# The FFN's block of a Mamba layer accumulated onto its rows by ScalarE, with B, C and dt stored sooner at a chunk's end

## What is computed

```
u    = layernorm(x);  xi, z = split(u @ in_proj)             # 1024 -> 2 x 2048
xc   = silu(causal_conv4(xi))
dt_r, B, C = rmsnorm of the three parts of xc @ x_proj       # 64, 16, 16
dt   = softplus(dt_r @ dt_proj + dt_bias);  A = -exp(A_log)
h_t  = exp(dt_t * A) * h_(t-1) + dt_t * B_t * xc_t           # 2048 channels x 16 states
y    = (sum_n h_t * C_t + D * xc) * silu(z)
x    = x + y @ out_proj.T                                    # 2048 -> 1024
x    = x + layernorm(x) @ W.T + bias                         # W = scale * (code - 128), 32 codes a scale
```

## Time and profile before

| what | value |
|---|---|
| median of 3 runs | 4584.67 us (4584.44 to 4585.98) |
| the profiled execution | 4594.81 us |
| its span, first to last instruction | 4593.0 us |
| a middle step (places 2 to 6), first scan to first scan | 32.26 us |
| place 7 and place 0 at the edge from chunk 7 to chunk 8 | 36.45 us and 38.77 us |
| wx, wo and wz loads | 1024 KB each, one of each in a step |

### The profile page before, as it was taken

One profiled execution on the slowest core, in us unless ns is written; L12 is line 12 of the kernel. 1 busy time (PEld: TensorE's weight loads), 2 busy tenths in 40 slices (PEclk: granted clock), 3 DMA queues, 4 the chain that ended last, 5 costly groups with the idle time before them and its releaser, 6 DMA issues.

```text
span 4593.0 us, 77871 instructions
## 1 busy us (share of the span) xinstructions
PE 4293.4 (93%) x25632; PEld 3867.8 (84%) x25632; DVE 4157.9 (91%) x5745; ACT 3535.6 (77%) x8848; POOL 3887.0 (85%) x2894
## 2 busy tenths in 40 slices
PE   7688889999999999999999999999999999998879
PEld 6567778888888988889888898988988888897769
DVE  3898989989999999999999899999999999999871
ACT  3787788878888788787878778787888878887750
POOL 0898989989898898989889898998989899899870
PEclk9788999999999999999999999999999999998889
DMA  7545556565756657575575756657575665655442
GB/s 245 159 126 175 151 181 177 167 216 173 220 160 189 194 174 221 155 220 168 165 230 156 225 163 208 187 153 229 163 222 172 199 182 162 213 172 177 136 141 92
DMA packets 201348, 828.91 MB, mean 180 GB/s; under 512 B 25456, under 2 KB 34416, under 8 KB 151792
## 3 DMA queue, kind: packets, MB, share of 16 engines
q1 hardware_dynamic: 141296, 639.35, 38.6%
q0 software_dynamic: 41216, 151.01, 18.7%
q10 hardware_dynamic: 18432, 33.56, 1.9%
HBM read 634.57 MB, written 55.05 MB: 150 GB/s over the span
## 4 chain that ended last, share of the span: by engine, by line
PE 61%; POOL 19%; DVE 8%; issue 7%; DMA 2%; ACT 1%; SPq 1%; POOLq 0%; DVEq 0%; ACTq 0%
PE ys L646 14%; PE gx L626 12%; POOL dbx L494 12%; PE ys L606 12%; PE g L799 10%; PE g L721 7%; DVE hb L1416 5%; POOL half L518 3%; POOL half L512 3%; PE ys L636 1%; PE hb L901 1%; DMA b_scratch<-ssmT 1%; DVE gx L1298 1%; DMA ybuf<-in_wf_scales 1%; POOL hd L507 1%
## 5 line engine op out<-in xcount | busy, mean ns | idle before, releaser
L494 POOL TENSOR_TENSOR dbx<-dtx,bb 128x1024 f32<-128x1024 f32 x1024 | 2426.6, 2370 | 232.3 <-DVE hb L1416 184.0
L1416 DVE TENSOR_TENSOR_SCAN hb<-hb,dbx 128x512 f32<-128x512 f32 x2048 | 2497.0, 1219 | 43.7 <-POOL dbx L494 25.7
L1111 ACT ACTIVATE hb<-dt,a_neg 128x256 f32<-128x256 f32 x4096 | 1789.1, 468 | 66.3
L606 PE MATMUL ys<-half,ident 128*128 128x256 f32 x3072 | 832.6, 407 | 186.4 <-POOL half L512 105.3
L799 PEld LDWEIGHTS g<-wo,ybuf 128*128 128x128 f32 x7680 | 945.0, 198 | 34.3 <-issue 17.7
L799 PE MATMUL g<-wo,ybuf 128*128 128x128 f32 x7680 | 953.2, 281 | 8.4 <-issue 8.4
L646 PE MATMUL ys<-xnT,wz 128*128 128x256 f32 x4096 | 925.2, 385 | 5.2 <-DVE ybuf L1375 5.2
L626 PE MATMUL gx<-xnT,wx 128*128 128x256 f32 x3968 | 894.4, 383 | 24.7 <-issue 10.8
L646 PEld LDWEIGHTS ys<-xnT,wz 128*128 128x128 f32 x4096 | 782.8, 193 | 116.0 <-DVE ybuf L1375 10.8
L606 PEld LDWEIGHTS ys<-half,ident 128*128 128x128 f32 x3072 | 580.5, 200 | 330.8 <-POOL half L512 138.2
L626 PEld LDWEIGHTS gx<-xnT,wx 128*128 128x128 f32 x3968 | 748.7, 191 | 129.3 <-issue 14.3
(11 more groups left out here) (108 smaller groups left out, 3134.7 us busy)
## 6 DMA issues: line engine op xcount, KB each, us to landing
wz<-in_win SPq DMA_DIRECT2D x128, 1024.0 KB, 5.0
hd<-hd POOLq DMA_DIRECT2D x256, 512.0 KB, 5.2
wx<-in_win SPq DMA_DIRECT2D x124, 1024.0 KB, 5.0
wo<-in_wout SPq DMA_DIRECT2D x123, 1024.0 KB, 7.3
wf<-wf_scratch SPq DMA_DIRECT2D x113, 512.0 KB, 3.6
xc_scratch<-xcn ACTq DMA_DIRECT2D x128, 256.0 KB, 2.8
xcs<-xc_scratch SPq DMA_DIRECT2D x128, 256.0 KB, 5.2
bb<-bc_scratch SPq DMA_DIRECT2D x64, 512.0 KB, 8.6
```

The costliest lines, as they stand in the source:

```text
L494: nc.gpsimd.tensor_tensor(dbx[:, k % 2, :].rearrange("p (n t) -> p n t", n=NQ), dtx[:, S % 2, a, :].unsqueeze(1).to_broadcast([P, NQ, T]), ...
L606: mm = nc.tensor.matmul(ys[i // 3][:, 0:T], ident[:], half[:, n % PLACES, w * T:(w + 1) * T], start=False, stop=(i % 3 == 2 and w == 1), s ...
L1111: ins = nc.scalar.activation(h[:, m * T:(m + 1) * T], dt[:, j % 2, a, :], ACT.Exp, scale=a_neg[:, ds((2 * j + a) * N + 2 * v + m, 1)])
L1416: nc.vector.tensor_tensor_scan(h[:], h[:], dbx[:, k % 2, w * UW:(w + 1) * UW], 0.0, ALU.mult, ALU.add).then_inc(scans, 1)
```

## The change

Four things change together.

1. In place 7 the RMS norm's square and sums, and ScalarE's evacuation of dt, B and C, stand one or two units earlier. TensorE makes `out_proj(3)` and `dt_proj` ahead of `x_in_proj(1)` and the groups. SyncE stores and loads B and C ahead of the load of wx, which waits for `x_in_proj(1)`.
2. In place 0 each part of the output block waits for the y of its own channel tiles, no longer for all 16. The parts 0 and 1 stand between late group 3 and late groups 4 and 5; VectorE makes the last y of the chunk before after product 3 (before: after product 1), and the first of its own after product 12 (before: 11).
3. The FFN's block is accumulated onto its rows: ScalarE copies the block's rows (x2 with the bias) into g1 after unit 15 (`ffn_in`, semaphore `f_pre`), TensorE accumulates onto them, and ScalarE copies the result out in the next step after unit 3 (`ffn_out`, semaphore `f_out`). VectorE's add (`add_ffn`) is gone, except for the last two chunks' at the kernel's end.
4. In the middle places TensorE's order is as before.

```diff
@@ SyncE
-                        sp.wait_ge(f_add, after(PAIRS * (c - 2)))
+                        sp.wait_ge(f_out, after(PAIRS * (c - 2)))
                         sp.dma_start(out_rows[c - 3], x2_rows(1 - st.parity)).then_inc(out_st, 16)
...
-                    if nx.x_job(nx_last):
-                        load_pair(S + PAIRS + 2)
                     if last and st.inproj:
                         bc_rows(c + 1)
                         for q in range(2):
                             load_b(c + 1, q)
                             load_c(c + 1, q)
+                    if nx.x_job(nx_last):
+                        load_pair(S + PAIRS + 2)
@@ TensorE
                     def g1_after_f():
-                        pe.wait_ge(f_add, after(S - 2 * PAIRS))
+                        pe.wait_ge(f_out, after(S - 2 * PAIRS))
...
-                        if was.outproj:
-                            g1_after_o()
-                        else:
-                            pe.wait_ge(f_add, after(S - 1 - 2 * PAIRS))
+                        pe.wait_ge(f_pre, after(S - 2 * PAIRS))
                         for tt in range(TT):
                             for kk in range(KH):
                                 mm = nc.tensor.matmul(g1[:, tt * P:(tt + 1) * P], x2nT[:, kk, tt * P:(tt + 1) * P],
-                                                      wf[:, kk, :], start=(kk == 0), stop=(kk == KH - 1))
+                                                      wf[:, kk, :], start=False, stop=(kk == KH - 1),
+                                                      skip_group_check=True)
...
-                            if first:
-                                pe.wait_ge(y_ready, after(2 * c * PAIRS))
                             if was.ffn:
                                 g1_after_f()
                             else:
                                 g1_after_o()
+                        if first:
+
+                            pe.wait_ge(y_ready, after(2 * (c - 1) * PAIRS + (part + 1) * TILES // 4))
...
                     ffn()
-                    late_groups()
+                    if first and st.ffn:
+                        late_groups(3)
+                        out_proj(0)
+                        out_proj(1)
+                        late_groups(4, 5)
+                    else:
+                        late_groups(3, 4, 5)
@@ ScalarE
+            def ffn_out(S):
+
+                k = S - 2 * PAIRS
+                act.wait_ge(f_mm, after(k))
+                nc.scalar.copy(block_rows((k - 1) // PAIRS, (k - 1) % PAIRS), g1_block).then_inc(f_out, 1)
+
+            def ffn_in(S):
+
+
+                k = S - 2 * PAIRS
+                act.wait_ge(bias_acc, 16 * (k // PAIRS + 1))
+                act.wait_ge(o_add, after(S - PAIRS + 1))
+                nc.scalar.copy(g1_block, block_rows(k // PAIRS, k % PAIRS)).then_inc(f_pre, 1)
...
+                    if st.before(first).ffn:
+                        ffn_out(S)
                     silus()
...
                     norm1(1)
+                    rms_square()
...
                     norm1(3)
-                    rms_square()
...
                     unit(10)
+                    ss_out()
...
                     unit(11)
                     norm2(3)
-                    ss_out()
...
                     unit(15)
+                    if st.ffn:
+                        ffn_in(S)
@@ VectorE
-                    add_ffn()
                     scan(2)
                     product(1)
-                    late_y()
+                    if not (first and st.ffn):
+                        late_y()
                     scan(3)
                     product(2)
+                    if last:
+                        add_x_proj()
                     scan(4)
                     product(3)
+                    if first and st.ffn:
+                        late_y()
                     scan(5)
                     product(4)
-                    add_x_proj()
+                    if last:
+                        rms_sums()
+                    else:
+                        add_x_proj()
                     scan(6)
                     product(5)
-                    rms_sums()
...
                     product(11)
-                    y_gate(S, 0)
+                    if not (first and st.ffn):
+                        y_gate(S, 0)
...
                     product(12)
+                    if first and st.ffn:
+                        y_gate(S, 0)
                     add_out()
```

## The result

The changed kernel takes **4618.1 us** (median of 4 runs, 4615.0 to 4623.0) against 4584.6 before: ratio 1.0075, 95% interval 1.006 to 1.009. The forecast was 4588, no change; the time is 2 us outside its range and on the slower side.

What follows compares the result with a forecast made beforehand. No single engine was held to bound the kernel; two nearly equal loops, over ScalarE and TensorE, set the middle step. Terms +19.5, +12, -22, -2.5 and -2 gave +5, shaded by 2: 4588 us, range 4552 to 4616.

Steps and rivals of the forecast that it cites:

- ScalarE's copies: Places 1 to 6, chunks 2 to 14: two new copies add 0.25 us to each of 78 steps, +19.5 us.
- less 0.07 and GpSimd's 0.21: Middle step, second loop: slacks of ScalarE and GpSimd taken off the table load's 0.47 us delay, leaving 0.2.
- the first loop: Middle step, over ScalarE: exponentials 3, table load, exponentials 4, scan 4, product freeing unit 3's bank; grows by 0.24 us.
- Place 7: Chunk edge: TensorE's z projection waits for VectorE's gate, +0.9 us at each of 13 edges, +12 us.
- Place 0: Start of chunk: fewer waits win 3.2 us, the clock's fall takes 1.5; -1.7 us at 13 edges, -22 us.
- wo lands late: Rival, places 7 and 0: wx ahead of wo in full DMA queues leaves place 0 worth 0; 4612 us, chance 0.28.
- the point named: Place 0: wo decides once it lands after 2302.2, 3.8 us into the place; from there each us costs one.
- The clock holds: Rival, place 0: shorter TensorE waits keep the clock up, giving the full -3.2 us; 4570 us, chance 0.22.
- VectorE was the bound: Rival, middle steps: each of 78 steps loses 0.33 us instead of gaining 0.25; 4544 us, chance 0.14.
- The third sign of being wrong: Place 0: a ScalarE wait for the bias transfer, with VectorE behind it; the wait was costed at nothing.
- The last edge: Edge from chunk 14 to 15: -2 us, with chunk 15 and the end staying as they are.
- The 10 us between trace and median: Kernel before: profiled execution 4594.81 against median 4584.67; the difference of 10.1 us was taken to stay the same.

Runs made afterwards that it cites:

- the run that takes the waits away: The changed kernel with wo loaded ahead of wx in place 7: 4606.6 us, ratio 1.0054 to the kernel before.
- the second: The kernel before, unchanged, traced once more: 4583.1 us, ratio 1.0002, span 4575.4 us.

## Why the prediction was wrong, step by step

**ScalarE's copies (+19.5 forecast, +37.5 measured): the step that failed.** The copy's time was right (0.37 estimated, 0.372 measured), and so was the wait for the FFN ("2103.01, 0.47 after the load's old start"). Wrong were the slacks taken off it: "less 0.07 and GpSimd's 0.21". 0.47 without them is within 0.03 of the growth. The 0.07 was the gap between unit 4's exponentials and scan 4, 0.12 in that step, less a hand-over of 0.04; but 0.10 us is that gap also in the changed kernel, where scan 4 plainly waits for ScalarE, and in no step of either trace is it smaller. At this scan it is the hand-over itself, although the gap comes down to 0.03 at scans of other units. The 0.21 was scan 9's end to GpSimd's next product less 0.13; this gap is 0.34 before and 0.35 after in middle steps, although the step grew by 0.5. It was no slack: GpSimd could not have followed sooner, as it was in its own work.

```profile
2116.60 1.27 POOL L518 TENSOR_TENSOR half<-hc 128x512 f32<-128x512 f32 x1
2117.82 2.37 POOL L494 TENSOR_TENSOR dbx<-dtx,bb 128x1024 f32<-128x1024 f32 x1
```

Its fold ends at 2117.87 and the product overlaps it by 0.05. From its transfer of hd at 2109.51 on, 0.30 us behind the end of product 3, GpSimd works without a wait over 0.1 us; after the change the same transfer stands 0.30 behind product 3 too. So scan 4 and product 3 hand their delay to GpSimd in full. The 0.06 of overlap taken off the copy in the first loop did not come either: the load of before began 0.02 behind the end of the exponentials, and that of now 0.01 behind the end of the copy.

VectorE's add leaving gave nothing, since it lay outside the loop. Here the result was right and the reason half right: VectorE did not wait anyway between unit 3 and scan 4 but for 0.16 us at the gate, and what makes the add free is that this gate waits for GpSimd's folds and TensorE's groups, which the add is not ahead of (0.47 us of wait after it). The page "Perfetto Trace Analysis" of the Trainium skill, section "Optimizing Scalar/DVE Operations", by whose rule, as the prediction read it, the step would have fallen with VectorE's work, is not borne out by this trace: VectorE's busy time fell by 0.24 us, and the step rose by 0.5. The measured growth alone would have put the sum at about +23 and the forecast at 4606, inside the range; the last edge and place 0, below, carried the time out of it.

**Place 7 (+0.9 forecast).** The order's own price is 0.77 us (0.8 in the working), measured twice (36.62 to 37.39, 36.39 to 37.16), with the forecast wait for the gate. The copies cost about 0.2 us here (36.39 with the sooner rows, 36.62 with the copies too), where the working had 0.1. It had nothing for the sooner rows, which give back 0.3 (36.71 to 36.39). Together this is +0.4 to +0.7.

**Place 0 (-1.7 forecast, -0.6 to -1.4 measured).** Counted from the start of the place the chain came out as worked out: scan 4 at 8.5 us (8.5), the x_proj add at 12.3 (12.4), wo at 3.5 (3.3), the wait for the row 2.30 us (2.2), with the clock at 0.95 or 0.96 in eight of 13 edges, 0.91 in one and 1.00 in four. (The sign "near 4.7 us after the first scan" for the output block counted from the old start of the place; by the working it was 3.6, and 3.74 was measured in chunk 8.) But the gain was credited to the wrong part. What wins are the B and C rows and the small row of first states arriving sooner, with which GpSimd's waits of 2.8 to 5.6 us ahead of the place go (4.25 in chunk 8); they were not in the working at all. Place 0 takes 37.45 us with the copies and the narrower wait for y alone, and 36.65 once the sooner rows and place 7's order are there. TensorE's and VectorE's new order there has a price of some 0.75: the 36.65 are with the old order in place 0, and the whole change has 37.40.

**The rivals.** "wo lands late" happened, in nine edges of 13, but not at a us for each us: in chunk 5 wo landed 4.7 us into the place, 0.9 behind the point named, and scan 4 came 0.4 later than in chunk 8; its own price, from the run that takes the waits away, is about 10 us (ratio 1.0075 to 1.0054, with intervals that touch). It gave 4612, nearest to the result, but for a sum in which the copies were still half their size. "The clock holds" did so in four edges of 13, and these still took 35.7 to 37.3 us, against the 35.6 of the prediction. "VectorE was the bound" is refuted by the gate's wait, which took up what the add left, and fits no run: with the copies alone the step grew to 32.76. The third sign of being wrong, a wait for the bias transfer in place 0, came in two edges, 2.6 and 0.5 us; behind the first VectorE waited 0.85.

**The last edge (-2 forecast, +6.4 measured).** The working said that chunk 15 stays as it is. In it there is no x_in_proj to keep TensorE busy until the gate, which now stands behind product 12: 6.49 us of wait, after which VectorE waits 6.44 in place 1. With the gate's old place chunk 15 gets some 3.5 us back. Some 2.5 more go with the copies (267.8 with the copies alone, 268.2 with them and the old order of place 0, 265.6 before).

**The 10 us between trace and median** were held to be a constant. They are not, so that differences from the first trace are too small by what its clock lost: the spans differ by +20 from the first trace and by +38 from the second, the medians by +33.5.

Left open: whether the narrower wait for y is all that makes place 0 0.6 us or more shorter with the copies alone. The fall of the clock differs between executions, and one trace each doesn't separate the two. Open, too, is how the 27 us of the sooner rows divide between the small row, B and C, dt and this wait.

## What to carry to other kernels

A constant minimum gap between a releaser and what it releases is a hand-over, not slack: look for the smallest value that it takes at this same instruction in all steps before subtracting it, and look whether the engine behind the gap is at work on something else. When an engine loses work, look at its next wait: if that grows by as much, the work was free. Follow the small transfers too: the edit that started a store of 0.1 KB, a load of 8 KB and the B and C rows sooner was worth more (27 us, with the narrower wait for y) than any order of the matmuls, and the profile named another releaser for the wait. Before an instruction is moved, list who waits for it in every place, and try the last iteration by itself, since it lacks the work that hides a wait elsewhere.

## What the runs showed of the hardware

On ScalarE a table load starts only behind the end of the copy before it (2101.06 and 2101.07) or of the exponentials before it (2102.52 and 2102.54 in the kernel before), while activations that follow each other mostly overlap by some 0.06 us. A 128x256 copy from PSUM takes 372 ns and one into PSUM 355. A store of 0.1 KB lands 4.6 us after its issue next to 1 MB of weights and 1.4 where no weights are under way. Two executions of one kernel can differ by 18 us with equal middle steps (spans of 4593.0 and 4575.4 us), most of it where the granted clock differs.
